# Joining the two halves of a head's output on VectorE, one word per choice in the dispatched row, and an earlier place for the zero fill

## The chip, the cores and the metric

The kernel runs on one core of one Trainium2 chip. The time is device microseconds of one execution; the median of the runs is what is compared. Engines are named as the profile names them: PE (TensorE), DVE (VectorE), ACT (ScalarE), POOL (GpSimd), SP (SyncE, which here only issues DMAs).

## The reference, cut to what matters

One transformer layer in float32: attention over 2048 tokens of 512 features, then a mixture of experts, each with a residual and a layer norm.

```python
# attention: 8 heads of 64 features, SCALE = sqrt(8)
q, k, v = x @ Wq + bq, x @ Wk + bk, x @ Wv + bv          # (2048, 512) each
weights = softmax(einsum('bdsh,bdth->bdst', q, k) / SCALE)
feats   = einsum('bdst,bdth->bdsh', weights, v)          # joined to (2048, 512)
x = layernorm(x + feats @ Wo + bo)
# experts: E = 64, TOPK = 6, CAP = 256 rows per expert
shared = (silu(g_s) * y_s) @ w_shared_down
scores = sigmoid(x_flat @ w_gate); topk_idx, w = top 6, w / w.sum
x_disp[e, place] = x_flat[token]        # place: how many rows the expert already has; over 256: dropped
out_r  = (silu(g_r) * v_r) @ w_down[e]
x = layernorm(x + shared + sum over the 6 of w * out_r[e, place])
```

## The kernel before, in words

To keep float32 precision at PE's faster formats, each operand is split into a high part (rounded by ACT, `..._hi`) and a low part (the rest, subtracted by DVE or POOL, `..._lo`), and products are made of the parts.

**Projections.** PE makes k (8 pieces), q (8) and v (8) in three PSUM slots that it goes round. For each q piece ACT writes `q_hi`, DVE writes `q_lo` (L956), and SP stores both to `q_hbm` (L449). ACT writes piece n only after the store of piece n - 2 has landed (L754).

**Attention.** The queries are cut into NCH = 8 chunks of 256, with H = 8 heads in each, and a head takes four steps. In a step s PE turns a quarter of the probabilities of step s - LAG (L1381), makes scores (L1394) and multiplies with v (L1419, one step later still). DVE subtracts the low parts (`p_lo`, L1133) and copies the scores out of PSUM with the row minimum (`prob`, L1158, which ends with an accumulator read); ACT makes the exponentials (L833) and the high parts (L816); POOL makes every fourth low part (L657). The order on each engine is the order of the loop; work that comes once per chunk (`chunk_end`) is put between by counters (`side_step`). PE may start to turn step r + 2 only when DVE has copied the scores of step s out, since both use the same slot (`wait_bank`).

`q_stack` holds the q of a head; SP loads that of head m + 2 when the scores of head m are done (L458, `load_q`), in its own queue behind whatever it has issued or waits to issue.

**The end of a head.** v is kept with its high part in columns 0 to 63 and its low part in columns 64 to 127, so the product `pv_acc` holds a head's output as two halves of 64 partitions that have to be added. DVE multiplies with the inverse row sums (L1141, `scaled`, 128 partitions). SP moves the lower half up with a DMA (L515, `moved`), POOL adds the halves (L675). For an even head the sum goes straight into `feats[0:64]`; for an odd head it goes into `moved`, and a second DMA carries it to `feats[64:128]` (L521). ACT and DVE wait for it with `head_out` before they write `scaled` again, and PE waits for heads 6 and 7 of a chunk before it multiplies with Wo (`out_project`, L1307).

**The end of a chunk.** Residual (POOL adds its bias, L590), layer norm, scores of the experts, choice of six, place in the expert. Each row is sent to `disp_hbm` by six indirect DMAs of POOL (L605). A row is the 512 features, the six chosen experts as floats, and six words `SKIP - (output row)` that POOL copies in (L591): WITH = 524 words.

**Zero fill.** `disp_hbm` is filled with zeros by 64 pieces of 524 KB from SP: Z_EARLY = 24 in a row behind the first two `load_q` (L466), the other 40 one per step from step 8 on (L531). The first scatter waits for all 64.

**Experts.** Items of 256 rows: 8 for the shared expert, 64 for the others. `load_rows` fetches rows, PE turns them, ACT and DVE split them, PE makes both products, and POOL scatters the results to `y_hbm` with row numbers from `row_at` (L699). DVE finds the row number with three instructions: `hit` (L1186: choice == expert, times the word), `found` (L1190, sum) and `row_at` (L1192). At the end the six results of each token are gathered and added.

`rows`, `sup_w` and others share memory with `k_stack`, and so are loaded during the last chunk, behind `head_used`.

Of the kernel before, what the change touches and what calls it, by code (L numbers as in the profile page):

```python
# [7 lines left out]
F32 = mybir.dt.float32  # L8
# [28 lines left out]
def build(nc, x, x_t, Wq, bq, Wk, bk, Wv, bv, Wo, bo, w_gate, w_sup, w_sdown, w_up, w_down, out):  # L37
# [16 lines left out]
    WITH = C + 2 * TOPK  # L54

    ctx = ExitStack()
    with ctx:
# [20 lines left out]
        to_skip = sb("to_skip", [P, NT, TOPK])  # L78
        zeros = sb("zeros", [P, WITH // 2])
# [60 lines left out]
        class Routing:  # L140


            def __init__(self, name):
                small = sb(f"small{name}", [P, 19], F32, att)
                self.top_sum = small[:, 0:1]
                self.place, self.over, self.slot_f = (small[:, 1 + TOPK * i:1 + TOPK * i + TOPK] for i in range(3))
# [38 lines left out]
        hit = [sb(f"hit{i}", [P, 2, TOPK]) for i in range(2)]  # L185
        found = [sb(f"found{i}", [P, 2]) for i in range(2)]
# [21 lines left out]
        v_resid, v_norm = sem("dve_resid"), sem("dve_norm")  # L208
# [4 lines left out]
        a_diag, p_comb, v_rowat, g_ids = sem("act_diag"), sem("pe_combined"), sem("dve_row_at"), sem("pool_ids")  # L213
# [5 lines left out]
        d_moved, d_feats, d_st, d_st_late = (sem(f"dma_{n}") for n in ("moved", "feats", "x1_store", "x1_store_late"))  # L219
# [98 lines left out]
        NZ, Z_EARLY = T * TOPK // (2 * P), 24  # L318
# [41 lines left out]

        def choices_of(c, j):
            return sent_of_chunk(c, j)[:, C:C + TOPK]
# [17 lines left out]
        def load_rows(e, n):  # L380
            b = n % NB
            if n >= NS:
                o = n - NB
                e.wait_ge(p_flip, o + 1)
                if o < NS:
                    e.wait_ge(v_base, o + 1)
                else:
                    e.wait_ge(v_rowat, 3 * (o - NS) + 1)
# [4 lines left out]
            else:  # L393
                head_used(e, n // 2)
# [27 lines left out]
        def sync(e):  # L422
# [42 lines left out]
            for g in range(Z_EARLY):  # L465
                e.dma_start(disp_pieces[g], zero_row).then_inc(d_zero, 16)  # L466
# [14 lines left out]
            def load_resid(c, j):  # L481
                if c == END:
                    head_used(e, (NS - 1) // 2)
# [5 lines left out]
            def load_for_shared(s):  # L489

                if s in (6, 10, 14):
                    for n in (0, 1):
                        load_rows(e, (s - 6) // 2 + n)
                elif s == 19:
                    for j in range(QT):
                        load_resid(END, j)
                elif s == 22:
# [10 lines left out]
            for s in range(LAST + LAG + 2):  # L508
# [9 lines left out]
                mj, uj = divmod(s - LAG - 2, STEPS)  # L518
                if mj >= 0 and uj == STEPS - 1 and mj % 2:
                    e.wait_ge(g_join, mj + 1)  # L520
                    e.dma_start(feats[D:P, (mj % H) // 2, :], moved[0:D, :]).then_inc(d_feats, 16)  # L521
# [8 lines left out]
                elif 2 * STEPS <= s < 2 * STEPS + E - Z_EARLY:  # L530
                    e.dma_start(disp_pieces[Z_EARLY + s - 2 * STEPS], zero_row).then_inc(d_zero, 16)  # L531
# [33 lines left out]
        def gpsimd(e):  # L565
# [8 lines left out]
            e.iota(to_skip[:, :, :], [[-P * TOPK, NT], [-1, TOPK]], base=SKIP, channel_multiplier=-TOPK,  # L574
# [12 lines left out]
            def bias_resid(c, j):  # L587
# [3 lines left out]
                e.tensor_copy(sent_of_chunk(c, j)[:, C + TOPK:WITH], to_skip[:, 2 * c + j, :]).then_inc(g_ids, 1)  # L591
# [10 lines left out]
            def scatter(c, j, k):  # L602
                if k == 0:
                    e.wait_ge(g_ids, 2 * c + j + 1)
# [47 lines left out]
            for s in range(LAST + LAG + 2):  # L652
# [14 lines left out]
                if s - END * H * STEPS in (25, 27):  # L667
                    bias_resid(END, (s - END * H * STEPS - 25) // 2)
# [891 lines left out]
```

## Time and profile before

| | us |
|---|---|
| median of 3 runs (1383.33 to 1386.36) | 1386.29 |
| the profiled execution | 1376.4 |
| its span | 1374.7 |
| PE busy in the span | 1275.5 |
| DVE busy | 1070.5 |
| POOL busy | 573.3 |

The span runs from the first to the last instruction. Busy time of PE counts overlapping matmuls once, so a PE that is busy all the time has no gaps, but isn't at its peak. The stages are: projections to 145 us, attention to 980, shared expert to about 1046, experts to 1294, the gather after that.

### The profile page before, as it was taken

The page shows a single profiled execution, that of the slowest core. Times are in us where ns is not written, and L with a number is a line of the kernel's source. Part 1 is how long each engine was busy: PE and PEld are TensorE (multiplying, and loading weights), DVE is VectorE, ACT ScalarE, POOL GpSimd, SP SyncE. Part 2 cuts the span into 40 slices and gives each one's busy share as a digit, 9 for nine tenths or more (in the row PEclk, how much of TensorE's full clock was granted, in tenths as well). Part 3 has the DMA queues.
Part 4 walks back from the last instruction along what each step waited for, and adds up shares of the span by engine and source line. Part 5 has one row for each costly group of instructions (what it writes and reads, how often), then busy time and mean ns, then how long its engine had stood idle before and what let it go on. Part 6 is the DMA issues. An engine that isn't in the chain of part 4 may idle for free. (4 is left out here: it accounts for less than half of the span.)

```text
span 1374.7 us, 24517 instructions
## 1 busy us (share of the span) xinstructions
PE 1275.5 (93%) x8128; PEld 1061.9 (77%) x8128; DVE 1070.5 (78%) x2070; ACT 899.0 (65%) x1639; POOL 573.3 (42%) x580
## 2 busy tenths in 40 slices
PE   7999599899999999999999999899898999999596
PEld 6888499789889889889889899688776777777332
DVE  5523478679979889889889889689677889999376
ACT  6412388668878778778778778678524566666242
POOL 0003122224524534434434434434443788888411
PEclk9999899999999999999999999999999999999899
DMA  6049989962324423424324324444438899997597
GB/s 233 36 197 221 222 194 206 202 163 86 119 69 131 142 75 123 136 81 130 123 85 134 117 83 134 146 143 157 157 125 296 290 357 349 356 357 268 217 422 303
DMA packets 151834, 253.72 MB, mean 185 GB/s; under 512 B 15507, under 2 KB 95507, under 8 KB 149280
## 3 DMA queue, kind: packets, MB, share of 16 engines
q1 hardware_dynamic: 131488, 197.04, 47.6%
q0 software_dynamic: 17920, 50.91, 9.7%
q10 hardware_dynamic: 2304, 4.20, 0.8%
q8 instruction: 69, 1.13, 0.4%
q14 instruction: 53, 0.43, 0.1%
HBM read 119.15 MB, written 135.07 MB: 185 GB/s over the span
## 5 line engine op out<-in xcount | busy, mean ns | idle before, releaser
L816 ACT ACTIVATE p_hi<-slot 128x512 fp32r<-128x512 f32 x512 | 278.2, 596 | 125.8 <-PE slot L1381 122.7
L657 POOL TENSOR_TENSOR p_lo<-prob,p_hi 128x512 fp32r<-128x512 f32 x128 | 166.1, 1297 | 432.7 <-ACT prob L818 432.4
L1394 PE MATMUL slot<-k_stack,q_stack 128*128 128x512 f32 x1024 | 301.4, 416 | 17.1 <-DMA q_stack<-q_hbm 15.2
L833 ACT ACTIVATE prob<-prob,row_min 128x1024 f32<-128x1024 f32 x256 | 296.8, 1159 | 0.4 <-DVE prob L1158 0.2
L1133 DVE TENSOR_TENSOR p_lo<-slot,p_hi 128x512 fp32r<-128x512 f32 x384 | 251.2, 682 | 56.5 <-ACT p_hi L816 55.1
L1419 PE MATMUL pv_acc<-p_hi,v_pair 128*128 128x256 f32 x1024 | 264.8, 292 | 6.7 <-POOL p_lo L657 5.7
L1381 PE MATMUL slot<-ident,prob 128*128 128x128 f32 x2048 | 265.3, 272 | 1.3 <-ACT prob L833 1.3
L1419 PE MATMUL pv_acc<-p_lo,v_pair 128*128 128x256 f32 x1024 | 254.1, 281 | 0.0
L1381 PEld LDWEIGHTS slot<-ident,prob 128*128 128x128 f32 x2048 | 230.0, 141 | 2.0 <-issue 1.7
L1419 PEld LDWEIGHTS pv_acc<-p_hi,v_pair 128*128 128x128 f32 x1024 | 193.3, 189 | 20.9 <-issue 11.3
L1394 PEld LDWEIGHTS slot<-k_stack,q_stack 128*128 128x128 f32 x1024 | 173.5, 190 | 42.6 <-DMA q_stack<-q_hbm 15.4
L1419 PEld LDWEIGHTS pv_acc<-p_lo,v_pair 128*128 128x128 f32 x1024 | 193.3, 189 | 12.6 <-issue 3.3
L1158 DVE TENSOR_SCALAR_CACHE_REDUCE prob<-slot 128x1024 f32<-128x1024 f32 x128 | 155.5, 1215 | 15.4 <-PE slot L1394 15.4
L1158 DVE TENSOR_SCALAR_CACHE_REDUCE prob<-slot,row_min 128x1024 f32<-128x1024 f32 x128 | 163.2, 1276 | 0.5 <-issue 0.2
L699 POOL DMA_INDIRECT y_hbm<-y_out,row_at x128 | 125.2, 978 | 42.4 <-issue 33.0
L850 ACT ACTIVATE rows_hi<-slot 128x1024 fp32r<-128x1024 f32 x72 | 73.8, 1027 | 49.5 <-PE slot L1447 49.5
L1181 DVE TENSOR_TENSOR rows_lo<-slot,rows_hi 128x1024 fp32r<-128x1024 f32 x72 | 88.0, 1224 | 21.6 <-ACT rows_hi L850 20.6
L687 POOL TENSOR_TENSOR up_lo<-up_w,up_hi 128x512 fp32r<-128x512 f32 x64 | 81.7, 1307 | 26.9 <-ACT up_hi L857 26.6
L605 POOL DMA_INDIRECT disp_hbm<-resid,scat x84 | 83.4, 993 | 21.0 <-issue 20.9
L1447 PEld LDWEIGHTS slot<-ident,rows 128*128 128x128 f32 x576 | 63.5, 141 | 33.5 <-issue 30.3
L1447 PE MATMUL slot<-ident,rows 128*128 128x128 f32 x576 | 76.3, 276 | 6.3 <-DVE y_out L1216 3.0
L818 ACT ACTIVATE prob<-slot 128x512 f32<-128x512 f32 x128 | 77.6, 606 | 0.0
(182 smaller groups left out, 2081.4 us busy)
## 6 DMA issues: line engine op xcount, KB each, us to landing
disp_hbm<-zeros SPq DMA_DIRECT2D x64, 524.0 KB, 9.9
rows<-disp_hbm SPq DMA_DIRECT2D x64, 524.0 KB, 6.2
y_hbm<-zeros SPq DMA_DIRECT2D x48, 512.0 KB, 3.4
got<-y_hbm SPq DMA_DIRECT2D x16, 1536.0 KB, 11.8
q_stack<-q_hbm SPq DMA_DIRECT2D x128, 128.0 KB, 3.9
up_w<-in_L_ffn_w_up SPq DMA_DIRECT2D x64, 256.0 KB, 5.4
down_w<-in_L_ffn_w_down SPq DMA_DIRECT2D x32, 256.0 KB, 6.6
q_hbm<-q_hi SPq DMA_DIRECT2D x8, 512.0 KB, 2.7
```

The lines of the kernel that those rows point to most:

```text
L605: e.indirect_dma_start(disp_hbm, bass.IndirectOffsetOnAxis(scat[j][:, k:k + 1], 0), sent_of_chunk(c, j), None, bounds_check=E * CAP - 1, o ...
L657: e.tensor_tensor(p_lo[1][:, 2:4, :], prob[:, m % 2, :, (4 * u + 2) * P:(4 * u + 4) * P], p_hi[1][:, 2:4, :].bitcast(F32), ALU.subtract).t ...
L699: e.indirect_dma_start(y_hbm, bass.IndirectOffsetOnAxis(row_at[:, 2 * g + t:2 * g + t + 1], 0), y_out[y][:, t, :], None, bounds_check=T * ...
L816: e.activation(p_hi[b][:, two, :], view[:, two, :], ACT.Copy).then_inc(a_phi, 1)
L833: e.activation(keys, keys, ACT.Exp, bias=row_min[:, me % 2, j, 1:2], scale=-1.0, accum_out=row_sum[:, me % 2, j, half:half + 1]).then_inc( ...
L1133: e.tensor_tensor(p_lo[b][:, two, :], view[:, two, :], p_hi[b][:, two, :].bitcast(F32), ALU.subtract).then_inc(v_lo, 1)
L1158: e.tensor_scalar(prob[:, ms % 2, j, half * HALF:(half + 1) * HALF], slot_of_take("scores", s)[:, :], -1.0 / SCALE, first, ALU.mult, ALU.m ...
L1181: e.tensor_tensor(rows_lo[f % 2][:, :, :], slot_of_take("flip", f)[:, :].rearrange("p (k q) -> p k q", k=KC), rows_hi[f % 2][:, :, :].bitc ...
L1381: made = e.transpose(view[:, t, j * P:(j + 1) * P], prob[:, m % 2, j, (4 * u + t) * P:(4 * u + t + 1) * P], ident[:, :])
L1394: made = e.matmul(slot[:, n * BANK:(n + 1) * BANK], qs[:, part, j * P:(j + 1) * P], k_stack[:, ms % H, keys], start=part == 0, stop=part == 1)
L1419: made = e.matmul(pv_acc[:, 0:QC], v_pair[:, kt, mv % H, :], src[:, t, :], start=kt == 0 and part == 0, stop=kt == NT - 1 and part == 1)
L1447: made = e.transpose(view[:, k, t, :], rows[f % NB][:, t, k * P:(k + 1) * P], ident[:, :])
```

## The change

It has three parts.

1. DVE makes `scaled` with two instructions of 64 partitions. One reads the half that isn't wanted there and writes it, shifted by 64 partitions, to `moved`; the other scales the head's own half. For even heads POOL adds the two, without a DMA to wait for; for odd heads DVE adds them itself, into `feats[64:128]`. Both DMAs (64 + 32) and half of POOL's additions go.
2. Choice and output row go into one word, `expert * 2^14 + row + 2^21`, written as uint32 by one DVE instruction per tile (in `sum_top`), so WITH is 518; POOL's copies go. In the experts stage `xor` with the expert's own code and a minimum give the row: two DVE instructions in place of three. `rows` is smaller, and its loads in the last chunk move from steps 6, 10, 14 to 10, 14, 18, the residual's from 19 to 23 (POOL's bias from 25, 27 to 28, 30), the shared weights' from 22 to 24.
3. The zero pieces: 14 before the first q store, two behind each of the first seven q stores, 12 behind the first two `load_q`, the remaining 24 one per step from step 8.

```diff
-    WITH = C + 2 * TOPK
+    WITH = C + TOPK
+    CODE_E, CODE_0 = 1 << 14, 1 << 21
-        NZ, Z_EARLY = T * TOPK // (2 * P), 24
+        NZ, Z_EARLY = T * TOPK // (2 * P), 40
         def head_out(e, m):
-            if m % 2:
-                e.wait_ge(d_feats, 16 * (m // 2 + 1))
-            else:
-                e.wait_ge(g_join, m + 1)
+            e.wait_ge(v_join if m % 2 else g_join, m // 2 + 1)
# SP
+            def zero_disp(pieces):
+                for g in pieces:
+                    e.dma_start(disp_pieces[g], zero_row).then_inc(d_zero, 16)
+            zero_disp(range(0, 14))
             for n in range(8):
...
+                if n < 7:
+                    zero_disp(range(14 + 2 * n, 16 + 2 * n))
...
             load_q(0)
             load_q(1)
-            for g in range(Z_EARLY):
-                e.dma_start(disp_pieces[g], zero_row).then_inc(d_zero, 16)
+            zero_disp(range(28, Z_EARLY))
...
                 if mv >= 0 and uv == STEPS - 1:
-                    e.wait_ge(v_scaled, mv + 1)
-                    e.dma_start(moved[0:D, :], scaled[D:P, :]).then_inc(d_moved, 16)
...
-                if mj >= 0 and uj == STEPS - 1 and mj % 2:
-                    e.wait_ge(g_join, mj + 1)
-                    e.dma_start(feats[D:P, (mj % H) // 2, :], moved[0:D, :]).then_inc(d_feats, 16)
# POOL
-                if mj >= 0 and uj == STEPS - 1:
-                    e.wait_ge(v_scaled, mj + 1)
-                    e.wait_ge(d_moved, 16 * (mj + 1))
+                if mj >= 0 and uj == STEPS - 1 and mj % 2 == 0:
+                    e.wait_ge(v_scaled, 2 * mj + 2)
                     e.wait_ge(p_proj, 2 * (mj // H))
...
# DVE
-                    e.tensor_tensor(scaled[:, :], pv_acc[:, 0:QC], scaled[:, :], ALU.mult).then_inc(v_scaled, 1)
+                    at = rows_of_head(mv)
+                    other = slice(D - at.start, P - at.start)
+                    e.tensor_tensor(moved[at, :], pv_acc[other, 0:QC], scaled[other, :], ALU.mult).then_inc(v_scaled, 1)
+                    e.tensor_tensor(scaled[at, :], pv_acc[at, 0:QC], scaled[at, :], ALU.mult).then_inc(v_scaled, 1)
+                    if mv % 2:
+                        e.wait_ge(v_scaled, 2 * mv + 2)
+                        e.wait_ge(p_proj, 2 * (mv // H))
+                        e.tensor_tensor(feats[D:P, (mv % H) // 2, :], scaled[D:P, :], moved[D:P, :],
+                                        ALU.add).then_inc(v_join, 1)
# DVE, sum_top: the word
+                e.scalar_tensor_tensor(
+                    out=sent_of_chunk(c, j)[:, C:WITH].bitcast(U32), in0=own.top_f[:, :], scalar=float(CODE_E),
+                    in1=code_row[:, 2 * c + j, :], op0=ALU.mult, op1=ALU.add).then_inc(v_code, 1)
# DVE, experts: hit, found, row_at become
+                    e.tensor_scalar(hit[g % 2][:, :, :], rows[f % NB][:, :, C:WITH].bitcast(U32), CODE_0 + CODE_E * g,
+                                    None, ALU.bitwise_xor).then_inc(v_rowat, 1)
+                    e.wait_ge(v_rowat, 2 * g + 1)
+                    e.tensor_reduce(row_at[:, 2 * g:2 * g + 2], hit[g % 2][:, :, :], AX.X, ALU.min).then_inc(v_rowat, 1)
```

## Rows read from the trace of the kernel before

**Rows 1.** The page, section 1: busy us (share of the span) and instructions.
```profile
PE 1275.5 (93%) x8128; PEld 1061.9 (77%) x8128; DVE 1070.5 (78%) x2070; ACT 899.0 (65%) x1639; POOL 573.3 (42%) x580
```
**Rows 2.** Waits: who waited for whom, us in total, times, longest.
```profile
PE slot L1394 <- DMA q_stack<-q_hbm: 15.2, 1, 15.2
```
**Rows 3.** Timeline of SP and PE, 100 to 172 us: start, us, instructions merged.
```profile
107.39 48.37 SPq L466 DMA_DIRECT2D disp_hbm<-zeros  x24
155.80 3.13 SPq L458 DMA_DIRECT2D q_stack<-q_hbm  x2
...
170.81 1.65 PE L1394 MATMUL slot<-k_stack,q_stack 128*128 128x512 f32 x3 [15.17 <-DMA q_stack<-q_hbm]
```
**Rows 4.** Windows: stretch, its length, busy us of five engines, PEclk, DMA, GB/s.
```profile
62.00:101.00 39.00, 39.00 (x171) 31.62 (x170) 8.99 (x7) 7.81 (x7) 0.00 (x0) 1.00 0.48 189
110.00:155.00 45.00, 43.68 (x202) 35.29 (x201) 23.35 (x32) 15.61 (x28) 12.34 (x8) 1.00 1.11 227
160.30:174.00 13.70, 3.19 (x11) 2.81 (x12) 1.08 (x1) 0.00 (x0) 0.00 (x0) 0.50 1.10 233
180.19:213.79 33.60, 33.60 (x248) 31.48 (x247) 28.22 (x51) 30.29 (x57) 9.83 (x9) 1.00 0.92 209
213.79:261.53 47.74, 45.91 (x331) 42.06 (x329) 36.34 (x68) 39.67 (x75) 13.00 (x12) 1.00 0.96 202
261.53:282.56 21.03, 16.57 (x93) 12.61 (x91) 9.99 (x19) 10.60 (x21) 4.67 (x5) 0.92 0.88 192
367.49:383.48 15.99, 15.29 (x93) 11.94 (x91) 12.05 (x19) 10.21 (x19) 8.78 (x10) 1.00 0.47 161
772.25:788.14 15.89, 15.29 (x93) 11.94 (x91) 12.08 (x19) 10.21 (x19) 8.79 (x10) 1.00 0.50 162
803.24:873.06 69.82, 69.82 (x519) 65.13 (x517) 63.98 (x137) 61.19 (x117) 28.11 (x28) 1.00 0.35 111
873.06:895.69 22.63, 18.09 (x93) 13.02 (x91) 12.05 (x19) 10.21 (x19) 8.72 (x10) 0.85 0.49 161
946.71:961.04 14.33, 13.22 (x99) 11.94 (x96) 14.19 (x24) 11.12 (x24) 9.11 (x10) 1.00 0.55 185
```
**Rows 5.** Timeline of POOL, SP and PE where chunk 6 ends.
```profile
873.18 1.30 POOL L590 TENSOR_TENSOR resid<-resid,bo_all 128x512 f32<-128x512 f32 x1
873.51 0.49 SPq L515 DMA_DIRECT2D moved<-scaled  x1
879.08 0.53 SPq L521 DMA_DIRECT2D feats<-moved  x1
885.09 6.48 PE L1307 MATMUL misc<-wo_sb,feats 128*128 128x512 f32 x8 [4.00 <-issue]
```
**Rows 6.** Timeline of DVE and PE at the end of one odd head.
```profile
725.90 0.42 DVE L1141 TENSOR_TENSOR scaled<-pv_acc,scaled 128x256 f32<-128x256 f32 x1 [0.54 <-issue]
726.24 1.27 DVE L1158 TENSOR_SCALAR_CACHE_REDUCE prob<-slot,row_min 128x1024 f32<-128x1024 f32 x1
...
727.44 0.08 DVE L1158 DVE_READ_ACCUMULATOR prob<-slot,row_min 128x1 f32 x1
...
728.40 1.03 PE L1381 MATMUL slot<-ident,prob 128*128 128x128 f32 x8
```
**Rows 7.** Timeline of DVE: four instructions on alternating halves.
```profile
32.24 5.23 DVE L945 SCALAR_TENSOR_TENSOR k_stack<-slot,bias_k,k_stack 64x1024 fp32r<-64x1024 f32 x4
```
**Rows 8.** Lines by form, the same instruction: busy us, mean ns, idle before.
```profile
L945 DVE SCALAR_TENSOR_TENSOR k_stack<-slot,bias_k,k_stack 64x1024 fp32r<-64x1024 f32 x16 | 20.5, 1283 | 12.1 <-ACT k_stack L742 11.8
```
**Rows 9.** Timeline of DVE: two small instructions beside a busy POOL.
```profile
950.06 2.43 DVE L1169 TENSOR_TENSOR row_inv<-row_sum 128x2 f32<-128x2 f32 x1
...
1058.19 3.13 DVE L1192 TENSOR_SCALAR row_at<-found 128x2 uint32<-128x2 f32 x1
```
**Rows 10.** Timeline of POOL in the experts stage, one pair to the next.
```profile
1156.75 0.99 POOL L699 DMA_INDIRECT y_hbm<-y_out,row_at  x1 [0.17 <-issue]
...
1164.30 1.00 POOL L699 DMA_INDIRECT y_hbm<-y_out,row_at  x1 [0.17 <-issue]
```

More of the change, by code:

```diff
@@ L77, in build @@
         ident = sb("ident", [P, P])
-        to_skip = sb("to_skip", [P, NT, TOPK])
-        zeros = sb("zeros", [P, WITH // 2])
+        code_row = sb("code_row", [P, NT, TOPK])
+        zeros = sb("zeros", [P, ZW])
         weight_of = sb("weight_of", [P, NT, TOPK])
@@ L143, in __init__ @@
             def __init__(self, name):
-                small = sb(f"small{name}", [P, 19], F32, att)
+                small = sb(f"small{name}", [P, 1 + 4 * TOPK], F32, att)
                 self.top_sum = small[:, 0:1]
-                self.place, self.over, self.slot_f = (small[:, 1 + TOPK * i:1 + TOPK * i + TOPK] for i in range(3))
+                self.top_f, self.place, self.over, self.slot_f = (
+                    small[:, 1 + TOPK * i:1 + TOPK * i + TOPK] for i in range(4))
                 self.score = sb(f"score{name}", [P, E], F32, att)
@@ L184, in build @@
         row_at = sb("row_at", [P, 2 * E], U32)
-        hit = [sb(f"hit{i}", [P, 2, TOPK]) for i in range(2)]
-        found = [sb(f"found{i}", [P, 2]) for i in range(2)]
+        hit = [sb(f"hit{i}", [P, 2, TOPK], U32) for i in range(2)]
         NG, BY_PE = 4, 3
@@ L218, in build @@
         d_qst, d_q = [sem(f"dma_q_store{i}") for i in range(2)], [sem(f"dma_q{i}") for i in range(2)]
-        d_moved, d_feats, d_st, d_st_late = (sem(f"dma_{n}") for n in ("moved", "feats", "x1_store", "x1_store_late"))
+        d_st, d_st_late = sem("dma_x1_store"), sem("dma_x1_store_late")
         d_scat = [sem(f"dma_scatter{j}") for j in range(2)]
@@ L666, in gpsimd @@
                     bias_resid((s - 43) // 32, 1)
-                if s - END * H * STEPS in (25, 27):
-                    bias_resid(END, (s - END * H * STEPS - 25) // 2)
+                if s - END * H * STEPS in (28, 30):
+                    bias_resid(END, (s - END * H * STEPS - 28) // 2)
                 mj, uj = divmod(s - LAG - 2, STEPS)
-                if mj >= 0 and uj == STEPS - 1:
-                    e.wait_ge(v_scaled, mj + 1)
-                    e.wait_ge(d_moved, 16 * (mj + 1))
+                if mj >= 0 and uj == STEPS - 1 and mj % 2 == 0:
+                    e.wait_ge(v_scaled, 2 * mj + 2)
                     e.wait_ge(p_proj, 2 * (mj // H))
-                    target = moved[0:D, :] if mj % 2 else feats[0:D, (mj % H) // 2, :]
-                    e.tensor_tensor(target, scaled[0:D, :], moved[0:D, :], ALU.add).then_inc(g_join, 1)
+                    e.tensor_tensor(feats[0:D, (mj % H) // 2, :], scaled[0:D, :], moved[0:D, :],
+                                    ALU.add).then_inc(g_join, 1)
                 side_step(jobs)
@@ L1015, in choose @@
                 e.wait_ge(done, at + 4)
-                e.tensor_copy(choices_of(c, j), own.top_i[:, 0:TOPK]).then_inc(done, 1)
+                e.tensor_copy(own.top_f[:, :], own.top_i[:, 0:TOPK]).then_inc(done, 1)
             def mark(c, j):
@@ L1023, in mark @@
                     own.onehot[:, :, :], iota_e[:, :].unsqueeze(1).to_broadcast([P, TOPK, E]),
-                    choices_of(c, j).unsqueeze(2).to_broadcast([P, TOPK, E]), ALU.is_equal).then_inc(done, 1)
+                    own.top_f[:, :].unsqueeze(2).to_broadcast([P, TOPK, E]), ALU.is_equal).then_inc(done, 1)
             def mark_any(c, j):
@@ L1062, in find_slots @@
                                 ALU.mult).then_inc(done, 1)
-                e.scalar_tensor_tensor(out=own.slot_f[:, :], in0=choices_of(c, j), scalar=float(CAP),
+                e.scalar_tensor_tensor(out=own.slot_f[:, :], in0=own.top_f[:, :], scalar=float(CAP),
                                        in1=own.place[:, :], op0=ALU.mult, op1=ALU.add).then_inc(done, 1)
@@ L1184, in vector @@
                 if f >= NS and f < NI:
-                    g, own = f - NS, rows[f % NB]
-                    e.scalar_tensor_tensor(
-                        out=hit[g % 2][:, :, :], in0=own[:, :, C:C + TOPK], scalar=float(g),
-                        in1=own[:, :, C + TOPK:WITH], op0=ALU.is_equal, op1=ALU.mult).then_inc(v_rowat, 1)
-                    e.wait_ge(v_rowat, 3 * g + 1)
-                    e.tensor_reduce(found[g % 2][:, :], hit[g % 2][:, :, :], AX.X, ALU.add).then_inc(v_rowat, 1)
-                    e.wait_ge(v_rowat, 3 * g + 2)
-                    e.tensor_scalar(row_at[:, 2 * g:2 * g + 2], found[g % 2][:, :], -1.0, float(SKIP), ALU.mult,
-                                    ALU.add).then_inc(v_rowat, 1)
+                    g = f - NS
+                    e.tensor_scalar(hit[g % 2][:, :, :], rows[f % NB][:, :, C:WITH].bitcast(U32), CODE_0 + CODE_E * g,
+                                    None, ALU.bitwise_xor).then_inc(v_rowat, 1)
+                    e.wait_ge(v_rowat, 2 * g + 1)
+                    e.tensor_reduce(row_at[:, 2 * g:2 * g + 2], hit[g % 2][:, :, :], AX.X, ALU.min).then_inc(v_rowat, 1)
                 side_step(jobs)
```

39 lines of the change are left out of this document (20 added, 19 removed).

## The prediction, made before the result was known

> **What bounds the kernel now.** I read section 1 of the page first: PE is busy 1275.5 of 1374.7 us [rows 1], so what can be gained outside the experts is mostly PE's idle time and its slow clock. The waits say where it idles: the largest single one is for `q_stack`, 15.2 us, once [rows 2]. The timeline puts it at 155.6 to 170.8. SP issued 24 zero pieces in a row over 48.4 us, and the loads of the next q came only at 155.80, behind the pieces still on their way [rows 3]. The windows show the rest [rows 4]. They run from the end of one head to that of another. Heads 0 to 3 take 33.60 us, 11.20 a head with PE always busy. The next four take 47.74, and the one that holds the end of chunk 0 takes 21.03. Where nothing waits, a chunk's end has 15.29 us of PE work; the second and the sixth take 15.99 and 15.89 (first and last of five alike). The seventh takes 22.63. Its timeline [rows 5] shows why: the first DMA of the join was issued at 873.51, POOL could add only after its own queue, the second DMA went out at 879.08, and PE started the product with Wo at 885.09, having idled 4.0 us; the clock of that window is 0.85. In the experts stage it is POOL that never rests: a pair of experts takes 7.55 us, four scatters and two subtractions end to end [rows 10].
>
> **The change part by part.** Sums are against the profiled execution, 1376.4 us (span 1374.7). The timed runs lie at 1386.3, 9.9 above; I apply the same difference to both kernels.
>
> *The wait for q, gone.* SP now reaches the load for head 2 with 12 pieces behind the first two loads, not 24. A piece costs 524 KB at 227 GB/s = 2.3 us while the DMA engines are saturated (from 110 to 155 us [rows 4]). If the first two loads go out at about 115 (below), 12 pieces end at about 143, before PE has finished the four score steps (about 148) that this load waits for. It lands some 4 us later, PE wants it at 155.6. So 15.2 us go, and with them the slow clock behind the idle time: from 160.3 to 174.0 it was 0.50 (the 1.2 GHz level), with 3.2 us of work in it [rows 4], so 1.6 us. Together 16.8.
>
> *The DMAs of the join, gone.* Chunk 0: 47.74 - 4 x 11.20 = 2.9, and 21.03 - 15.6 = 5.4 (0.3 us left for a late low part of POOL). Its zero pieces saturated the DMAs that joined the halves; now no join uses one, and the single pieces end at step 31 rather than 47. Chunk 6: 22.63 - 15.6 = 7.0, gap and clock. The five between: 5 x 0.35 = 1.8. Together 17.1. What is late next at a chunk's end is PE itself.
>
> *What DVE gets.* It is the price of the above. `scaled` took 0.42 us and the next instruction started 0.34 behind it [rows 6]. The new ones have 64 partitions and 256 columns each; by columns they last as long, 0.42. Whether they overlap is the question. Four instructions that alternate between the halves took 5.23 us, 1.31 each [rows 7], where one lasts 1.28 [rows 8]: no overlap, 0.03 us between them. I take that for the new ones, as the row nearest in kind. Even heads: 2 x 0.45 - 0.34 = +0.56. Odd heads, with the addition: 3 x 0.45 - 0.34 = +1.01. With overlap it would be +0.34 and, since the addition waits for its inputs, about +0.8. Over 64 heads DVE gets 32 x 1.57 = 50 us.
>
> The Trainium skill states the first case as a rule ("VectorE: DVE Perf Modes", section "Two Vector instructions with no wait between them"): an instruction whose operands start in another 32-partition quadrant than the last ones waits until all earlier ones have finished. By it the stalls below are 6 us, without it under 1; the 1.31 against 1.28 agrees with it.
>
> How much of the 50 is seen? DVE has room: from the end of head 49 to that of 55 it is busy 63.98 of 69.82 us [rows 4], and 3 x 1.57 = 4.7 more makes 68.7. But behind `scaled` stands the copy of the scores, and PE's next-but-one turn waits for that: copied at 727.52, used at 728.40, a slack of 0.88 [rows 6], of which I leave 0.1 for the signal (an estimate; no row isolates it). Even heads fit, odd heads miss by 0.2 to 0.25. Taken for three odd heads of four (in the fourth PE has a chunk's work in between), 24 x 0.25 = 6 us. Ends: nothing, and all 50.
>
> One of these additions, head 7 of each chunk, meets POOL's bias (L590 began 0.1 us after `scaled` [rows 5]). Small DVE instructions beside a busy POOL took 2.43 us and 3.13 us where their work is 0.2 [rows 9], so it can cost about 0.5 us seven times; it falls where PE then waits for POOL anyway (the 0.3 above), and I count nothing more. The last chunk is tighter: DVE is busy 14.19 of 14.33 us between heads 60 and 61 [rows 4], so nothing hides there: +1 for two or three heads.
>
> *The zero pieces between the q stores.* SP is idle there until `q_lo` is made. The first 14 pieces need 32 us of the stretch from 26 us (when the weights have landed) to 62. From 62 to 101 seven intervals of 5.57 us carry a pair of stores each at a DMA share of 0.48 [rows 4]; against the saturated 1.11 that is 2.4 us. With two pieces, 7.0 us in 5.57: a backlog of 1.5 an interval, 10 us at the last store, which lands at about 115 in place of 104. ACT may write q piece n when store n - 2 has landed: about 5 us of slack at first, so the last pieces come 1 to 2 us late, and PE, with three slots, doesn't notice. The loads for heads 0 and 1 need to land by 131. Cost taken: nothing; with the cover gone, 10.
>
> *Waits added.* DVE's addition waits for `p_proj`; behind it stand all of DVE's steps, but for head 1 of a chunk the product asked for is several steps old. POOL's first scatter waits for the code word, written steps before. Nothing.
>
> *Codes and rows.* One DVE instruction of about 0.2 us more per tile, 16 in all, in the shade; in the last chunk 0.3 us, neglected. In the experts DVE saves about 0.2 us per item, where POOL bounds: nothing. But before POOL is saturated, `row_at` was held up twice, for 3.13 us in the one of two alike that is shown [rows 9], and POOL's pairs came 2 us later each time. That instruction goes; its successor, `xor`, stands where `hit` stood. I take 3 of about 4.4. Ends: 4.4 gained, and 4.4 lost if `xor` is caught instead.
>
> The Trainium skill has the mechanism ("SBUF — State Buffer", section "Who interferes with whom"): VectorE and GpSimd share a port pair, and the second to ask waits for the whole instruction of the first; one-input instructions like `xor` can ask for it too. By that rule the 3 us is luck of position, and could as well be 0.
>
> **Sum.** -16.8 - 17.1 + 6 + 1 - 3 = -29.9: profiled 1346.5, timed about **1356 us**.
>
> **Rivals.**
> - *Halves overlap* (0.12). DVE is fast enough and the slack takes everything: 6 us less, 1350. Against it: rows 7 and 8.
> - *The zero pieces hold up q* (0.15). The backlog of 10 us reaches PE, because a store lands later than I think or the first loads slip past 131: 1366. For it: the DMA share has been 1.11 wherever zeros ran. Against: three PSUM slots of cover.
> - *Lock-outs in the experts* (0.08). `xor` is caught as `row_at` was, and the 3 isn't gained but 4.4 lost: 1363.
> - *DVE becomes the bound* (0.05). Place: every head's end; price up to 50 us. If stalls run round the ring of PE, ACT and DVE rather than being absorbed, all of it is seen: 1386 - 37 + 50 = 1399. It turns slower than before once three quarters of the 50 are exposed. For it: 68.7 of 69.8 us. Against: over those six heads PE has no gap at all [rows 4], so it has not once waited for DVE yet.
>
> **How the numbers follow.** Forecast 0.60, rivals as given. Range 1342 to 1371: low, overlap and 4.4 in the experts, with some of the 9.9 between timed and profiled gone too; high, the backlog and 5 us more of DVE. Below 0.3% (about 4 us) a change can't be told from none. Faster 0.93, same 0.02, slower 0.05.
>
> **What would show it.** No wait for `q_stack` over 1 us. Windows over a chunk's end at about 15.6 us, chunks 0 and 6 among them, without a clock under 1. The two half instructions 0.45 us apart, not 0.34. PE gaps of 0.2 to 0.3 before L1381 behind odd heads, none behind even. The last q store issued before 115 and PE without a gap to 148. POOL's pairs still 7.55 apart. Wrong would be: a head above 11.6 us in chunk 0 (DVE bounds), a gap of PE between 100 and 131 (q held up), or DVE instructions of 3 us at `xor`.

## The result, and the profile after

The changed kernel took 1373.76 us (median of 6 runs, 1369.45 to 1377.13), the kernel before 1384.81 beside it (1379.59 to 1387.95): a ratio of 0.992 (95% interval 0.9891 to 0.9949), 11 us less where 30 were forecast, and outside the range. In the later comparison of the two, in other runs, the changed kernel took 1371.42 and the kernel before 1372.14: 0.9999 (0.9985 to 1.0013). The changed kernel repeats to 0.2% in these two; the kernel before doesn't (1384.8, then 1370.4, 1372.1 and 1367.0 as medians of four comparisons), and why is not settled. The last three comparisons ran on three different chips, and no run separates the chip from the rest. So it is not settled either whether the change gains 11 us or nothing; both are far from the 30 that were forecast. Against its own profiled execution the change is small too: the span is 1372.6 us in place of 1374.7.

Section 1 of the page after, against [rows 1]:

```profile
span 1372.6 us, 24420 instructions
## 1 busy us (share of the span) xinstructions
PE 1282.8 (93%) x8128; PEld 1062.5 (77%) x8128; DVE 1105.9 (81%) x2118; ACT 905.2 (66%) x1639; POOL 550.4 (40%) x532
```

DVE has 48 instructions more and 35 us more busy. The table says where time came and went. It is made from the starts of ACT's `scaled` (one for each head) in the traces. "Head 4" or "the head at 4" is the stretch from that start for head 3 to that for head 4, so DVE's addition for head 3 falls in it. "Chunks 1 to 6" holds heads 1 to 7 of each, and an "end" runs from head 7 of a chunk to head 0 of the next. The second execution is that of the run after_again, below.

| us | before | after | after, second execution |
|---|---|---|---|
| to head 0 | 177.5 | 173.6 | 169.3 |
| chunk 0 with its end | 102.3 | 94.4 | 94.5 |
| chunks 1 to 6, seven heads each | 510.2 | 534.0 | 532.0 |
| ends of chunks 1 to 5 | 80.4 | 76.8 | 76.8 |
| end of chunk 6 | 22.5 | 15.4 | 15.4 |
| last chunk | 84.1 | 84.7 | 84.7 |
| last head to last scatter of the experts | 314.8 | 308.7 | 311.9 |
| from there to the end | 83.0 | 85.1 | 84.1 |

The ends gained what was forecast for them. Two things went wrong: the start, and 24 us in the middle of the chunks.

**The middle.** Windows of the changed kernel, heads 4, 6 and 7 of chunk 1 (columns as in [rows 4]); in the kernel before they lasted 11.36, 11.21 and 11.37 us with PE busy throughout:

```profile
306.56:319.34 12.78, 12.12 (x87) 10.65 (x86) 12.55 (x30) 10.21 (x20) 2.82 (x4) 1.00 0.07 22
331.95:344.46 12.51, 11.68 (x83) 10.39 (x82) 11.68 (x25) 10.25 (x21) 2.62 (x3) 1.00 0.18 63
344.46:356.69 12.23, 11.72 (x87) 10.61 (x86) 12.06 (x29) 10.21 (x20) 3.53 (x5) 1.00 0.27 88
```

PE idles 0.5 to 0.8 us in each, and its busy time is 0.8, 0.5 and 0.4 us longer for nearly the same matmuls. Lines by form of the changed kernel (count | busy us, mean ns) show the code word and an instruction that has grown:

```profile
L1039 DVE SCALAR_TENSOR_TENSOR resid<-small,code_row 128x6 uint32<-128x6 f32 x14 | 15.3, 1096 | 0.0
...
L1025 DVE TENSOR_TENSOR x_t<-iota_e,small 128x384 f32<-128x384 f32 x15 | 12.8, 852 | 0.0
```

The code word, six elements a row, takes 1.10 us on average where about 0.2 was forecast. The one-hot comparison (L1025, which marks a token's six experts in six rows of 64) takes 852 ns for 554 before. Others have shrunk: `row_inv`, at which [rows 9] showed 2.43 us, has gone from 477 to 246 ns on average (30.5 to 15.8 us in all), and `weight_of` from 488 to 152 ns. Timeline of the changed kernel, POOL, DVE and PE at one code word (start, us):

```profile
305.57 1.29 POOL L661 TENSOR_TENSOR p_lo<-prob,p_hi 128x512 fp32r<-128x512 f32 x1 [3.21 <-ACT prob L821]
305.63 0.09 DVE L1172 DVE_READ_ACCUMULATOR prob<-slot 128x1 f32 x1
305.63 1.26 DVE L1039 SCALAR_TENSOR_TENSOR resid<-small,code_row 128x6 uint32<-128x6 f32 x1
...
306.81 0.15 DVE L1042 TENSOR_REDUCE small<-top 128x1 f32<-128x6 f32 x1
...
307.07 0.67 DVE L1139 TENSOR_TENSOR p_lo<-slot,p_hi 128x512 fp32r<-128x512 f32 x1
...
307.89 1.15 PE L1404 MATMUL slot<-k_stack,q_stack 128*128 128x512 f32 x4 [0.49 <-DVE p_lo L1139]
```

POOL began its low part 0.06 us before DVE came to the code word, and DVE's instruction ended when POOL's did (306.86 and 306.89). The next `p_lo` is late, and PE waits for it. The one-hot of the second tile in the changed kernel, DVE and then POOL:

```profile
335.55 0.42 DVE L1154 TENSOR_TENSOR feats<-scaled,moved 64x256 f32<-64x256 f32 x1
336.01 1.28 DVE L1172 TENSOR_SCALAR_CACHE_REDUCE prob<-slot,row_min 128x1024 f32<-128x1024 f32 x1
337.22 0.08 DVE L1172 DVE_READ_ACCUMULATOR prob<-slot,row_min 128x1 f32 x1
337.22 1.22 DVE L1025 TENSOR_TENSOR x_t<-iota_e,small 128x384 f32<-128x384 f32 x1
```
```profile
336.74 1.29 POOL L661 TENSOR_TENSOR p_lo<-prob,p_hi 128x512 fp32r<-128x512 f32 x1 [4.42 <-ACT prob L821]
```

and at the same place of the kernel before, DVE and then POOL:

```profile
346.45 0.55 DVE L1022 TENSOR_TENSOR x_t<-iota_e,resid 128x384 f32<-128x384 f32 x1
```
```profile
347.00 1.30 POOL L657 TENSOR_TENSOR p_lo<-prob,p_hi 128x512 fp32r<-128x512 f32 x1 [4.42 <-ACT prob L818]
```

DVE used to be 0.55 us ahead of POOL here; with the join it comes 0.48 us behind. `p_lo` on DVE, whose first input lies in PSUM, took 0.63 to 0.69 us in all 384 instances, also in the 51 that began beside a low part of POOL.

**The start.** Timeline of SP, the last q stores of the changed kernel and what follows:

```profile
97.69 0.46 SPq L459 DMA_DIRECT2D q_hbm<-q_lo  x1
98.20 1.23 SPq L452 DMA_DIRECT2D disp_hbm<-zeros  x2
105.28 0.33 SPq L459 DMA_DIRECT2D q_hbm<-q_hi  x1
...
106.14 3.57 SPq L452 DMA_DIRECT2D disp_hbm<-zeros  x2
115.43 0.33 SPq L459 DMA_DIRECT2D q_hbm<-q_hi  x1
...
126.54 2.58 SPq L470 DMA_DIRECT2D q_stack<-q_hbm  x4
129.16 21.36 SPq L452 DMA_DIRECT2D disp_hbm<-zeros  x12
154.59 1.27 SPq L470 DMA_DIRECT2D q_stack<-q_hbm  x2
```

PE in the same kernel: the two gaps of the projections and the one at head 2's q:

```profile
105.31 0.50 PE L1255 MATMUL slot<-w_hi,x_hi 128*128 128x512 f32 x1 [1.31 <-DVE q_lo L959]
...
115.46 0.51 PE L1255 MATMUL slot<-w_hi,x_hi 128*128 128x512 f32 x1 [4.29 <-DVE q_lo L959]
...
166.78 1.78 PE L1404 MATMUL slot<-k_stack,q_stack 128*128 128x512 f32 x4 [3.37 <-DMA q_stack<-q_hbm]
```

Stores 5.6 us apart at first are 8 to 10 us apart at the end, the first loads of q go out at 126.5, and of the old wait of 15.2 us [rows 2] 3.4 are left. Behind the gap of 4.29 and behind that of 3.37 the granted clock was 0.50 for 3.4 us each; by the work in these stretches that is another 3.4 us (an estimate). In the second execution there was one gap of 1.2 us in the projections, and 3.5 us of waiting for q. The waits of the changed kernel name the link (us in total, times, longest):

```profile
ACT q_hi L758 <- DMA q_hbm<-q_lo: 32.3, 4, 9.0
```

### The profile page after: what moved, and what is told of

It reads as the page before. It is cut to its first block and busy times, and to the rows that moved or that the text cites. A ratio compares the mean times of both kernels' runs of the same rounds, so it can differ in the third digit from the quotient of the medians.

```text
span 1372.6 us, 24420 instructions
## 1 busy us (share of the span) xinstructions
PE 1282.8 (93%) x8128; PEld 1062.5 (77%) x8128; DVE 1105.9 (81%) x2118; ACT 905.2 (66%) x1639; POOL 550.4 (40%) x532
## 5 line engine op out<-in xcount | busy, mean ns | idle before, releaser
L1391 PEld LDWEIGHTS slot<-ident,prob 128*128 128x128 f32 x2048 | 229.5, 141 | 11.5 <-DVE prob L1172 9.6
L875 ACT ACTIVATE y_out<-slot 128x512 f32<-128x512 f32 x64 | 34.9, 595 | 64.6 <-PE slot L1503 64.6
```

Source lines behind the costliest of these rows:

```text
L1391: made = e.transpose(view[:, t, j * P:(j + 1) * P], prob[:, m % 2, j, (4 * u + t) * P:(4 * u + t + 1) * P], ident[:, :])
```

## The experiments

Two theories on the middle. *Lock-out*: a DVE instruction with both inputs in SBUF that meets a running POOL instruction is held until its end ("caught" below), and the change put two such instructions into POOL's way. *Load*: DVE's 50 us of added work are seen wherever they stand. On the start: the pieces between the stores hold up q, or they don't. Ratios are to the kernel before in the same comparison. Experiments 1 to 4 and 6 to 7 have no run of the changed kernel beside them, so their gains are read from the stretches of the traces.

**1. Zero pieces eased** (`zeros_eased`).

```diff
-        NZ, Z_EARLY = T * TOPK // (2 * P), 40
+        NZ, Z_EARLY = T * TOPK // (2 * P), 33
-            zero_disp(range(0, 14))
+            zero_disp(range(0, 16))
-                    zero_disp(range(14 + 2 * n, 16 + 2 * n))
+                    zero_disp(range(16 + n, 17 + n))
-            zero_disp(range(28, Z_EARLY))
+            zero_disp(range(23, Z_EARLY))
```

> The changed kernel with its zero pieces eased: 16 before the q stores (14), one between two stores instead of two, 10 behind the first loads of q (12), the other 31 (24) one a step. Theory (the pieces between the stores hold up q): the q stores stay 5.6 us apart and the eighth is issued by 103 us (115 in the changed kernel), PE has no gap between 100 and 131 us (5.6 us in two gaps), the loads of heads 0 and 1 go out by 107 (126.5), and the wait for q_stack at the first turn (3.4 us) goes too, since the 10 pieces behind them end by 135. Head 0 ends 7.8 us earlier, head 1 11 us; time about 1363. Rival 1 (the stall is the batch's or the weights' work, the pieces in between only coincide): stores stay late, at most 2 us are gained. Rival 2 (given back later): the single pieces, now to step 38, fall on the loads of q and of the first chunk's rows, heads 4 to 8 take over 0.5 us more each, and the time stays at about 1370.

Measured 1361.03 us, ratio 0.993 (0.9902 to 0.9958). Head 0 came at 161.0 us (173.6 and 169.3 in the changed kernel); PE has no gap for q. Timeline of SP:

```profile
95.94 0.43 SPq L459 DMA_DIRECT2D q_hbm<-q_lo  x1
96.42 0.79 SPq L452 DMA_DIRECT2D disp_hbm<-zeros  x1
101.14 0.32 SPq L459 DMA_DIRECT2D q_hbm<-q_hi  x1
101.50 0.43 SPq L459 DMA_DIRECT2D q_hbm<-q_lo  x1
105.46 2.58 SPq L470 DMA_DIRECT2D q_stack<-q_hbm  x4
108.08 15.12 SPq L452 DMA_DIRECT2D disp_hbm<-zeros  x10
147.15 1.75 SPq L470 DMA_DIRECT2D q_stack<-q_hbm  x2
```

A store of `q_hi` landed in 2.9 us (median) where the changed kernel's page has 9.3. Chunk 0 took 94.3 us, so nothing was given back there: the theory holds. It holds over all the traces too: head 0 came at 165.9 to 173.6 us in the six executions with the change's pieces, and at 160.7 to 161.6 in the five with the eased ones.

**2. Code word earlier** (`code_early`). The instruction moves from `sum_top` to the end of `choose`:

```diff
                 e.tensor_copy(own.top_f[:, :], own.top_i[:, 0:TOPK]).then_inc(done, 1)
+                e.wait_ge(done, at + 5)
+                e.scalar_tensor_tensor(
+                    out=sent_of_chunk(c, j)[:, C:WITH].bitcast(U32), in0=own.top_f[:, :], scalar=float(CODE_E),
+                    in1=code_row[:, 2 * c + j, :], op0=ALU.mult, op1=ALU.add).then_inc(v_code, 1)
```

> The changed kernel with the one DVE instruction that makes the code word moved from the step sum_top to the end of the step choose, right behind the cast it reads, where POOL has just ended its low part. Theory (lock-out: a DVE instruction with both inputs in SBUF that meets a running POOL instruction waits for its end): the code word takes 0.16 to 0.2 us in place of 1.25 in 11 of the 12 tiles of chunks 0 to 5; the heads at 4 in a chunk lose 1.2 of the 1.4 us that they are longer than in the kernel before, those at 7 lose the 0.9; gain 2 us a chunk, 12 us in all, time about 1362. The one-hot instruction of the second tile stays caught (1.22 us). Rival (DVE's added work as such, 50 us, costs the time): the same instructions in another place cost the same, time 1374 and DVE busy unchanged but for the stall.

Measured 1360.20 us, ratio 0.9922 (0.9894 to 0.9951). The code word took 0.17 us in all but the last tile (0.22). Chunks 1 to 6 took 526.1 us, 7.9 less than the first execution of the changed kernel and 5.9 less than the second: heads at 4 and 7 lost 0.6 and 0.7, not 1.2 and 0.9. That is lock-out, since no work was taken away, but part of head 4's excess is something else. The gain of 12 us that was expected didn't come. `scat`, which was 0.01 us behind the start of a low part wherever it was caught, took 1.30 us twice, as in the first execution of the changed kernel (in the second never); each time head 5 was 1.3 us longer. One of the two (the same kernel, DVE; POOL's low part began at 312.38):

```profile
312.20 0.16 DVE L1070 SCALAR_TENSOR_TENSOR small<-small 128x6 f32<-128x6 f32 x1
312.39 1.30 DVE L1074 TENSOR_TENSOR scat<-small 128x6 uint32<-128x6 f32 x1
```

**3. POOL adds once per pair** (`pair_add`).

```diff
-                    e.tensor_tensor(scaled[at, :], pv_acc[at, 0:QC], scaled[at, :], ALU.mult)...
-                    if mv % 2: ...                  # DVE's addition
+                    e.wait_ge(p_proj, 2 * (mv // H))
+                    e.tensor_tensor(feats[at, (mv % H) // 2, :], pv_acc[at, 0:QC], scaled[at, :], ALU.mult)...
# POOL, behind odd heads only
+                    both = feats[:, (mj % H) // 2, :]
+                    e.tensor_tensor(both, both, moved[:, :], ALU.add).then_inc(g_join, 1)
```

> The changed kernel without DVE's third instruction behind odd heads: the second half instruction writes into feats, and POOL adds moved to feats once per pair of heads, over 128 partitions. 32 instructions less on DVE (0.46 us each, 15 us), 32 additions on POOL for 32. Lock-out theory: behind the odd head DVE comes back to its old phase, so the one-hot instruction of each second tile is ahead of POOL's low part again (0.55 us for 1.22) and the heads at 6 lose 1.1 of their 1.3 us; the code word stays caught, so the heads at 4 and 7 stay long. With 0.3 us of every second head of chunk 0 that is 7 to 8 us, less about 0.3 us at each chunk's end where PE's product now waits for POOL: time about 1368. Load theory (each us on DVE is seen): 14 us less, 1360, with the heads at 4 and 7 shorter too.

ACT, too, waits for the half instructions and no longer for the join of the head before. Measured 1380.54 us, ratio 1.0069 (1.0047 to 1.0092): slower, against both theories. The cause is a wait that I added. DVE writes into `feats` already behind head 0, and so waits there for PE's product of the chunk before. Waits of this kernel:

```profile
DVE feats L1150 <- PE misc L1312: 33.3, 7, 4.8
```

Heads at 1 and 2 took 16.6 and 13.4 us (14.8 and 12.6). The one-hot was caught still, in 1.66 us: with one instruction less DVE came 0.04 us after POOL, no longer 0.48, but it was held all the same. The head start of 0.55 us is used up by even two half instructions. For the load theory speak heads 4, which lost 0.5 us, and chunk 0, 1.3; heads 6 and 7 lost nothing.

**4. All three edits** (`best3`).

> The three edits together (zero pieces eased, code word behind the cast, POOL's addition once per pair). If the three causes are apart, their gains add: 11 + 12 + 6 = 29 us less than the changed kernel, about 1345, and no head of chunks 1 to 5 is more than 0.3 us longer than in the kernel before. If they share a cause or PE's path takes over from DVE, less: 1352.

Measured 1365.34 us, ratio 0.9958 (0.9937 to 0.9978), 20 us over what was expected if the gains add: head 0 at 161.6 us and the code word at 0.17 as in 1 and 2, heads at 1 and 2 at 16.6 and 13.4 us by the wait of 3.

**5. The changed kernel and its parts, together** (`after_again`, `codes_only`, `zeros_back`, `join_back`). zeros_back takes back the zero pieces' lines of the diff ahead (24 in a row behind the first loads of q), join_back the join's, codes_only both:

```diff
-                    e.tensor_tensor(moved[at, :], pv_acc[other, 0:QC], scaled[other, :], ALU.mult)...
-                    e.tensor_tensor(scaled[at, :], pv_acc[at, 0:QC], scaled[at, :], ALU.mult)...
+                    e.tensor_tensor(scaled[:, :], pv_acc[:, 0:QC], scaled[:, :], ALU.mult).then_inc(v_scaled, 1)
# SP
+                    e.dma_start(moved[0:D, :], scaled[D:P, :]).then_inc(d_moved, 16)
+                    e.dma_start(feats[D:P, (mj % H) // 2, :], moved[0:D, :]).then_inc(d_feats, 16)
```

> The changed kernel itself, beside its parts on one chip: 0.992 of the time of the kernel before, as first measured (11 us less). Its attention stage (from the first head's end to the last's) 5.8 us longer than before's, head 0 about 4 us earlier.

> The kernel before with the second part of the change alone (one code word per choice; the join by DMAs and the zero pieces as before). Lock-out theory: what catches the one-hot and the code word is DVE's phase, which the join shifts; with the old join DVE reaches the second tile's one-hot 0.5 us ahead of POOL's low part and the step sum_top 0.26 us ahead of it, so they take 0.55 and 0.16 us, and no head of chunks 1 to 5 is over 0.3 us longer than before. Gain only in the experts, 4 to 6 us: ratio 0.996. Rival (the code word is caught wherever the join puts DVE): 1.25 us each, heads at 4 and 7 longer by 0.7 each, 9 us lost, ratio 1.002.

> The changed kernel with the zero pieces as before (24 in a row behind the first loads of q, none between the stores). The pieces between the stores cost 7.8 us and save 11.7: so head 0 ends 4 us later than in the changed kernel, with no gap of PE before 150 us and 15 us of waiting for q_stack, and the rest as in the changed kernel: 4 us slower, ratio to before 0.995. Rival: the single pieces, now to step 47, slow the first chunk's loads and the end of chunk 0 as before, 2 to 5 us more: ratio 0.998.

> The changed kernel with the join by DMAs of the kernel before (one DVE instruction a head, POOL's additions, two DMAs). Lock-out theory: heads at 4, 6 and 7 of chunks 1 to 5 fall back to 11.4, 11.2 and 11.4 us, 3.6 us a chunk or 20 in all; against it the ends of chunk 0 and chunk 6 wait for the DMAs again (5 and 7 us, and 1 us at each other end): net 4 to 8 us faster than the changed kernel, ratio to before 0.987. Rival (the join on DVE is worth its 17 us, and its work hardly costs): 10 us or more slower than the changed kernel, ratio 1.0.

| | join | zero pieces | us | ratio (95%) | to head 0 | chunk 0 | chunks 1 to 6 | ends 1 to 5 | end 6 |
|---|---|---|---|---|---|---|---|---|---|
| after_again | DVE | new | 1371.42 | 0.9999 (0.9985, 1.0013) | 169.3 | 94.5 | 532.0 | 76.8 | 15.4 |
| codes_only | DMAs | old | 1375.11 | 1.0030 (1.0009, 1.0051) | 181.7 | 103.4 | 511.2 | 79.4 | 16.8 |
| zeros_back | DVE | old | 1382.88 | 1.0084 (1.0063, 1.0105) | 179.9 | 94.5 | 534.1 | 76.8 | 15.4 |
| join_back | DMAs | new | 1354.63 | 0.9881 (0.9853, 0.9909) | 170.5 | 95.9 | 511.1 | 81.8 | 16.8 |

All four have the code word. With the old join it took 0.15 to 0.17 us in every tile but one (1.21), with the new one 1.23 to 1.26 in 11 of the 12 of chunks 0 to 5. Lines by form of the kernel of the run join_back:

```profile
L1049 DVE SCALAR_TENSOR_TENSOR resid<-small,code_row 128x6 uint32<-128x6 f32 x14 | 3.3, 236 | 0.0
```

So the instruction is cheap and its place is not what makes it dear: DVE's phase is, which the join shifts. Taking the join on DVE back gains 17 us. The zero pieces' part is worth 11 us (zeros_back against after_again), not the 4 expected: head 0 came 4.3 us earlier in after_again than in the first execution of the same kernel, and 2.4 us later in zeros_back than in the kernel before. Over all traces head 0 came at 177.5 to 181.7 us with the old pieces (three executions), so the new ones are worth 10.5 us there on average. join_back's ratio was expected (0.987), but by luck: it was to be 4 to 8 us faster than the changed kernel and was 16.8, and the expected ratio built on a gain of 11 us that didn't come back in this comparison. codes_only missed as a sum: the attention is as long as before to 1 us in chunks 1 to 6, as expected, but head 0 came 4.2 us later than in the kernel before, with 17.0 us of waiting for q. Read down the column of chunk 0: with the old pieces the join by DMAs costs 8.9 us there, with the new ones 1.4. Either part alone cures it.

The end of chunk 6 took 22.5 us in the kernel before and 16.8 in codes_only and join_back, whose join is the same. The traces say what the difference is. In the kernel before SP, between the two DMAs of the join [rows 5], issued the loads of `rows`, which the second part of the change moves from step 6 to step 10. Timeline of SP:

```profile
874.10 1.08 SPq L399 DMA_DIRECT2D rows<-x_hbm  x2
```

DMA issues of the kernel before (873.4 to 879.9 us), then of best7 (experiment 7; 858.5 to 864.5), which has the same join and the moved loads (KB each, median us from issue to landing):

```profile
rows<-x_hbm SPq DMA_DIRECT2D x2, 512.0 KB, 5.5
feats<-moved SPq DMA_DIRECT2D x1, 64.0 KB, 5.9
```
```profile
feats<-moved SPq DMA_DIRECT2D x1, 64.0 KB, 3.1
```

In both, POOL's addition and the second DMA come at the same place, 8.0 and 8.7 against 7.8 and 8.6 us behind head 7, so POOL's missing copy is not it. The DMA lands in 5.9 us beside the loads and in 3.1 without, PE idles 4.0 us and not 1.2, and then the granted clock is 0.50 for 6.8 us; in codes_only it stays at 1.00. No run moves the loads alone.

**6. Off POOL's beat** (`off_beat`). Only the steps of three pieces of routing change:

```diff
-                for n, part in enumerate((score_experts, choose, mark, mark_any, sum_top, share, pick_rank,
-                                          find_place, find_slots)):
-                    yield from clock(start + 6 + 2 * n)
+                for at, part in ((6, score_experts), (8, choose), (12, mark), (14, mark_any), (16, sum_top),
+                                 (16, share), (18, pick_rank), (20, find_place), (22, find_slots)):
+                    yield from clock(start + at)
```

> The changed kernel with the same DVE instructions, of which three stand in another step of the loop over heads: the one-hot and the maximum over it one step later, the code word and the sum one step later (each second step has a low part of POOL, which starts as DVE leaves the scores; now they fall in the steps between). Lock-out theory: one-hot 0.55 us and code word 0.16 us in every tile; heads at 6 and 7 of chunks 1 to 5 go back by 1.1 and 0.7 us, those at 4 by 0.7 of 1.4 (the rest is the third instruction behind odd heads): 2.5 us a chunk, 15 us in all, ratio to before 0.989. Rival (the work as such, wherever it stands): within 2 us of the changed kernel, ratio 1.0.

Measured 1349.36 us, ratio 0.9867 (0.9848 to 0.9886); chunks 1 to 6 took 518.9 us, 13.1 less than in after_again and 15.1 less than in the first execution of the changed kernel. Heads at 4, 6 and 7 of chunk 1 (windows of this kernel):

```profile
298.71:310.75 12.04, 11.80 (x86) 10.52 (x85) 11.78 (x29) 10.22 (x22) 2.89 (x4) 1.00 0.07 23
323.35:334.86 11.51, 11.40 (x84) 10.52 (x83) 10.68 (x25) 10.09 (x21) 2.60 (x3) 1.00 0.20 68
334.86:346.46 11.60, 11.60 (x86) 10.50 (x85) 11.40 (x29) 10.21 (x21) 3.58 (x5) 1.00 0.30 93
```

On average over chunks 1 to 6 the excess of these heads over the kernel before falls from 1.3, 1.3 and 0.85 us to 0.67, 0.31 and 0.22. One-hot and code word took 0.55 and 0.16 us there. Of the 8.7 us that are left over the kernel before, 7.2 are in these three heads, DVE's added work as such, and 1.3 are one caught `scat`. Over the twelve tiles of chunks 0 to 5 the code word takes 12.0 us less than in the changed kernel and the one-hot 4.0, and the chunks 15.1 less, so lock-out accounts for the gain. That the same work merely stands in other steps is not separated from it by this run.

**7. Three versions for use** (`best5`, `best6`, `best7`). best6 is the edits of 1 and 6. best5 adds POOL's one addition for the second to fourth pair of a chunk; the first pair stays as in the change, so the wait of experiment 3 never comes up. best7 is join_back with the edit of 1.

> Zero pieces eased, the steps moved as in the run off_beat, and POOL's addition once per pair of heads for the second to fourth pair of a chunk (the first pair as in the changed kernel, so that DVE never waits at head 0 for the product of the chunk before). Expected: 10 us from the zero pieces, 15 from the lock-outs, 3 to 4 from 24 DVE instructions less (heads at 4): 1343, ratio 0.979, and heads at 1 and 2 of a chunk at 14.8 and 12.6 us again (16.6 and 13.4 with the addition for every pair). Rival: POOL's addition, 0.3 us longer over 128 partitions, makes new meetings and gives 2 to 5 us back: 1347.

> Zero pieces eased and the steps moved, the join as in the changed kernel. If the gains add: 10 + 15 = 25 us less than the changed kernel, 1346, ratio 0.981.

> The join by DMAs of the kernel before with the code word and the eased zero pieces: 1354.6 - 10 = 1345, ratio 0.981, with code word and one-hot uncaught. Rival: the single zero pieces, now to step 38, hold up the joins of chunk 0 as in the kernel before (heads at 4 and 6 and the chunk's end 2 to 5 us longer): 1349, ratio 0.984.

best5: 1334.79 us, ratio 0.9765 (0.975 to 0.9781), better than both kernels and than expected. Windows, heads 4, 6 and 7 of chunk 1:

```profile
292.75:304.25 11.50, 11.50 (x86) 10.50 (x85) 11.20 (x28) 10.21 (x22) 3.59 (x5) 1.00 0.07 24
316.84:328.05 11.21, 11.21 (x84) 10.51 (x83) 10.40 (x25) 10.09 (x22) 3.28 (x4) 1.00 0.21 70
328.05:339.49 11.44, 11.44 (x86) 10.49 (x85) 11.24 (x28) 10.23 (x21) 2.90 (x4) 1.00 0.30 94
```

PE has no gap in any. Chunks 1 to 6 took 511.7 us, 1.5 over the kernel before: 8.3 less than best6 (520.0). Of the 8.3, 2.6 are two `scat` that were caught in best6 and not here; the other 5.7 came from 18 instructions of 0.46 us, 8.3 us of DVE time. That is the added work again. best6: 1344.70 us, 0.9837 (0.9821 to 0.9853), as expected from adding the gains. best7: 1347.79 us, 0.9857 (0.9834 to 0.9881); there the rival came true. Chunk 0 took 101.2 us, for the single pieces, now to step 38, meet the joins again (window of best7, the end of chunk 0):

```profile
240.69:261.96 21.27, 16.87 (x84) 12.11 (x83) 9.89 (x18) 10.09 (x19) 5.66 (x5) 0.84 0.61 141
```

## Why the prediction was wrong, step by step

- *The wait for q, 16.8 us*: 3.9 in the first execution of the changed kernel, 8.2 in the second, 10.5 on average over all traces with either placement. The failed step is "Cost taken: nothing; with the cover gone, 10". The last store was to land at 115; it was issued at 115.4 and q could be loaded at 126.5. A store took 9.3 us to land, ACT waited for one four times (32.3 us in all), `q_lo` and the next store behind it, so the lateness fed itself, and the slots were no cover: PE lost 5.6 us in two gaps in the first execution, and 1.2 to 1.8 in one gap in four of the five others. And then the batch of 12 started at 129, not at 115, so the load for head 2 was late by 3.4 us. The rival "the zero pieces hold up q" (0.15) was the right one.
- *The join's DMAs, 17.1 us*: chunk 0 gave 7.9 (8.3 forecast), chunk 6 7.1 (7.0), the five ends 3.6 (1.8). The sum was right, two of its reasons weren't, so that it came out is luck. In chunk 6, 5.7 us were lost not to the join by itself, nor to POOL's own queue as the prediction reads [rows 5], but to the loads of `rows` between its two DMAs, and the second part of the change, which moves them, gives these back with the old join too (codes_only; by the traces, for no run moves them alone). In chunk 0 the zero pieces' part alone would have done it (1.4 left). Undone on its own, the join by DMAs costs 1.4 + 5.0 + 1.5 us: 8, not 17.
- *DVE's stalls, 6 + 1 us*: 24 us, and 0.6 in the last chunk. Of the 24, 15 went with the moved steps (experiment 6), 7 are the added work and 1 is a caught `scat`. The work's price was close. The half instructions stand 0.45 and 0.46 us apart, as forecast. Where it shows was partly luck: not 0.25 behind three odd heads of four, but 0.3 behind three odd heads of chunk 0, and in chunks 1 to 6 0.67 and 0.31 behind heads 3 and 5, 0.22 behind head 6 and nothing behind head 1. The sign that was named, a head over 11.6 us in chunk 0, could not show the rest, for chunk 0 has no code word or one-hot beside its heads; the longest took 11.5.
- *The failed step* for the 15 us is "One DVE instruction of about 0.2 us more per tile, 16 in all, in the shade". It was put at nothing beyond its 0.2 us; it took 1.23 to 1.26 in 11 of 12 tiles. I asked what the instruction costs and not what POOL does when it runs, though [rows 9] showed two like it at 2.4 and 3.1 us. And I priced the join by DVE's time, not by the shift it gives to all that follows: the one-hot was 0.55 us ahead of POOL in the kernel before and 0.48 behind it in the changed one.
- The Trainium skill has the mechanism as a rule ("SBUF — State Buffer", section "Who interferes with whom"): a DVE instruction with two SBUF inputs contends with a GpSimd one that reads SBUF, one with at most one SBUF input (outside the two-port modes) doesn't. The traces agree: one-hot (1.22 us for 0.55), code word (1.25 for 0.16) and `scat` (1.30 for 0.17) were caught, `p_lo` from PSUM never (0.63 to 0.69). I had used the mechanism for the experts and for one addition a chunk (it took 0.82 us for 0.42 in six of them), and not for these.
- *Experts, 3 us*: 6.1 in the first execution, 2.9 in the second; over all 13 executions with the code word 4.6 on average (1.8 to 6.1). `row_at`'s 3 us went. `xor` is caught, 0.60 us on average and up to 1.18 in the first execution and 0.18 in the second (`hit` took 0.47), which the rival had; POOL's pairs stay 7.55 us apart on average, so it costs nothing.
- *What the sum left out*: the gather behind the last scatter, not changed, took 85.1 us for 83.0 in the first execution, 84.1 in the second.
- *The timed runs, 9.9 us over the profiled one*: that was the kernel before alone, in its first comparison. The changed kernel's median is 0.6 under its profiled execution (1374.34).

## What to carry to other kernels

An instruction that is moved or lengthened on an engine shifts the phase of all that follow it; list those that share a resource with another engine, and look in the trace by how much each is ahead of it. Where it is less than the shift, add the other engine's whole instruction to the price. A filler DMA behind a store that someone waits for has the price of that store's landing time (2.9 us with one piece, 9.3 with two), not of the bandwidth. And judge parts of a change by taking each away: here two parts cured the same stall in chunk 0 and two the one in chunk 6, and one of them cost 17 us net.

## What the runs showed of the hardware

- A DVE instruction of 128 x 6 elements with both inputs in SBUF took 0.15 to 0.17 us when it began before a low part of POOL or between two, and 1.19 to 1.30 us when it came 0.01 to 0.12 us after the start of one (1.29 us). The one-hot, 128 x 384, took 0.55, 1.22 when it came 0.48 us after the start, and 1.66 at 0.04 us.
- PE's gaps from this were 0.5 to 0.7 us, and the granted clock stayed at 1.00 in every window shown of chunk 1; in best7's window with 4.4 us of idling it was 0.84.
- A DMA of 64 KB landed in 3.1 us, and in 5.9 with two more of 512 KB ahead of it in the same queue.
